# A message-passing layer on one core: layer 3 computed with edges on partitions, and 60 blocks selected by one-hots in place of 52

## What is computed

```python
x_j, x_i = x[src], x[dst]                       # (200000, 32) each
msg = concatenate([x_i, x_j - x_i], axis=-1)    # 64 columns
h = relu(msg @ W1 + b1)                         # W1 64x64
h = relu(h @ W2 + b2)                           # W2 64x128
h = relu(h @ W3 + b3)                           # W3 128x64
m = h @ W4 + b4                                 # W4 64x32
s = segment_sum(m, dst, 12500)
out = layernorm(x + s / maximum(cnt, 1)[:, None])
```

## Time and profile before

| | us |
|---|---|
| timed runs, median (lowest to highest) | 1571.46 (1568.09 to 1571.53) |
| the profiled execution: span from first to last instruction | 2441.1 |
| TensorE matmul busy in it | 1767.5 |
| VectorE busy | 947.9 |
| ScalarE busy | 602.6 |
| GpSimd busy | 1125.9 |
| mean granted clock of TensorE | 0.764 of full speed |

### The profile page before, as it was taken

How to read it: one execution, slowest core, us unless ns; L and a number is a source line. 1 busy time by engine, 2 the same in 40 slices (tenths; PEclk the granted TensorE clock), 3 DMA queues, 4 the chain that set the end, 5 groups by cost and what they waited for, 6 DMA issues and landing times.

```text
span 2441.1 us, 39243 instructions
## 1 busy us (share of the span) xinstructions
PE 1767.5 (72%) x13131; PEld 1040.0 (43%) x13131; DVE 947.9 (39%) x3086; ACT 602.6 (25%) x945; POOL 1125.9 (46%) x1165
## 2 busy tenths in 40 slices
PE   3133777777768777878787778786867778777797
PEld 2112444444444444444444444444444444444454
DVE  3663343333333343333333333443333333333356
ACT  2233122222212222212222222222221222122234
POOL 5275444453544454354545454544444454444411
PEclk7555787877878787777778877777877877787888
DMA  5334643343434443353434353544344344444332
GB/s 128 98 93 88 200 112 112 106 140 94 136 101 116 126 121 109 103 147 91 135 105 136 104 152 92 152 109 114 104 123 115 111 114 109 133 118 118 109 106 59
DMA packets 189929, 283.06 MB, mean 116 GB/s; under 512 B 84614, under 2 KB 90169, under 8 KB 189156
## 3 DMA queue, kind: packets, MB, share of 16 engines
q1 hardware_dynamic: 152341, 241.67, 33.7%
q0 software_dynamic: 36704, 37.00, 7.3%
q10 hardware_dynamic: 682, 1.85, 0.3%
HBM read 266.51 MB, written 13.73 MB: 115 GB/s over the span
## 4 chain that ended last, share of the span: by engine, by line
PE 63%; issue 23%; another core or an unknown queue 6%; DVE 3%; ACT 2%; DMA 1%; SPq 1%; DVEq 0%; POOL 0%; ACTq 0%; POOLq 0%
PE ps L964 22%; PE ps L996 12%; PE ps L988 10%; PE ps L1019 5%; PE ps L1004 4%; PE ps L919 3%; PE ps L901 3%; PE ps L1016 2%; PE ps L978 2%; ACT work L716 1%; ACT work L731 1%; DMA sums<-in_src 1%; DVE region L1410 0%; DVE region L1292 0%
## 5 line engine op out<-in xcount | busy, mean ns | idle before, releaser
L585 POOL DMA_INDIRECT xj<-z_rows,src_t x1107 | 1074.5, 971 | 1190.9 <-PE ps L919 787.7
L964 PE MATMUL ps<-region,x_p 128*96 128x150 bf16 (+53 forms) x5876 | 569.6, 243 | 416.6 <-issue 407.2
L964 PEld LDWEIGHTS ps<-region,x_p 128*96 128x96 bf16 x5876 | 440.6, 142 | 572.9 <-issue 566.7
L731 ACT ACTIVATE work<-ps,b3s 128x512 f32<-128x512 f32 x196 | 134.7, 687 | 1335.5 <-PE ps L996 1037.1
L996 PE MATMUL ps<-work,w3s 128*64 128x512 f32 x784 | 356.6, 840 | 21.2 <-issue 21.1
L1377 DVE TENSOR_SCALAR region<-region,cst 128x1565 bf16<-128x1565 int16 (+6 forms) x416 | 245.7, 634 | 268.0 <-remote 256.3
L988 PE MATMUL ps<-work,w2s 64*128 64x512 f32 x784 | 298.1, 827 | 6.8 <-ACT work L716 5.6
L724 ACT ACTIVATE work<-ps,b2s 128x512 f32<-128x512 f32 x392 | 250.7, 684 | 161.0 <-PE ps L988 82.7
L1392 DVE COPY work<-ps 128x512 f32<-128x512 f32 x194 | 133.4, 687 | 336.4 <-PE ps L1004 217.0
L1386 DVE CAST work<-ps 96x512 bf16<-96x512 f32 x52 | 35.7, 686 | 513.9 <-PE ps L964 506.8
L1410 DVE TENSOR_SCALAR region<-iota_g,dst_rel 128x42 f32<-128x42 f32 x1120 | 185.7, 250 | 0.0
(11 more groups left out here) (156 smaller groups left out, 826.3 us busy)
## 6 DMA issues: line engine op xcount, KB each, us to landing
dstb<-dst_rows SPq DMA_DIRECT2D x196, 252.0 KB
region<-src_rows SPq DMA_DIRECT2D x104, 391.2 KB
region<-src_rows SPq DMA_DIRECT2D x52, 407.2 KB
region<-src_rows SPq DMA_DIRECT2D x52, 403.2 KB
region<-src_rows SPq DMA_DIRECT2D x52, 376.2 KB
region<-src_rows SPq DMA_DIRECT2D x52, 375.8 KB
region<-src_rows SPq DMA_DIRECT2D x52, 374.0 KB
region<-src_rows SPq DMA_DIRECT2D x52, 366.2 KB
```

The lines of the kernel that those rows point to most:

```text
L585: pool.indirect_dma_start(out=xj[:, u, j % UT, j // UT, 0:w], out_offset=None, in_=rows, in_offset=bass.IndirectOffsetOnAxis(ap=cols[:, j: ...
L964: chosen = nc.tensor.matmul(ps[0:XP, XBANK[h], lo - h * UE:hi - h * UE], xb[:, a, :], hot[:, q % QN, at + lo:at + hi], start=not begun[h], ...
```

## The change

Layer 3's matmuls have their operands exchanged: the block's h2 tile (128 features x 128 edges) is loaded and the 64 columns of W3 are moved, so the result has edges on partitions at once. Eight such matmuls stand in place of two with 512 moved columns and of the four turning matmuls. They write one of two banks, by the block's parity. The bias b3 is now along the free axis, where ScalarE cannot add it, so relu(a + b3) is written as max(a, -b3) + b3: VectorE's copy becomes a maximum with a row that holds -b3 on every partition, and b3 through W4 is added once to the last layer's bias row, which the counts multiply. ScalarE's relu 3 and its first copies go. One step of distance goes too: the sum is now of block s-2 in step s, the one-hots are built for block s-1, and the addition stands directly behind the maximum on VectorE. SB grows from 52 to 60.

```diff
-SB = 52
+SB = 60
...
-        p_x, p_h1, p_h3 = ps[:, 0, :], ps[:, 1, :], ps[:, 4, :]
+        p_x, p_h1 = ps[:, 0, :], ps[:, 1, :]
         p_h2 = ps[:, 2:4, :]
-        p_ht = ps[:, 5, :]
+        p_h3 = ps[:, 4:6, :].rearrange("p v (t h f) -> p v t h f", t=UT, h=2)
+        p_b4 = ps[H3:H3 + 1, 7, 256:256 + O]
...
# sync: -b3 comes to all partitions
+            sp.dma_start(floor3[:, :], b3.unsqueeze(0).to_broadcast([P, H3])).then_inc(s_w, 16)
...
# scalar
-            def relu3(s):
-                v = s % 2
-                act.wait_ge(s_l3, 2 * (s + 1))
-                if s >= 2:
-                    act.wait_ge(s_ht, s - 1)
-                nc.scalar.activation(h3[:, v, :], p_h3, ACT.Relu, bias=b3s[:, 0:1]).then_inc(s_r3, 1)
...
# tensor
             def layer3(s):
-                if s >= 1:
-                    pe.wait_ge(s_r3, s)
+                if s >= 2:
+                    layer3_copied(pe, s - 2)
                 for h in range(2):
                     pe.wait_ge(s_r2[h], s + 1)
-                    nc.tensor.matmul(p_h3[h * H3:(h + 1) * H3, :], w3s[:, :], h2[:, s % 2, h, :],
-                                     start=True, stop=True).then_inc(s_l3, 1)
+                    for t in range(UT):
+                        made = nc.tensor.matmul(p_h3[:, s % 2, t, h, :], h2[:, s % 2, h, t * T:(t + 1) * T], w3s[:, :],
+                                                start=True, stop=True)
+                made.then_inc(s_l3, 1)
-
-            def turn_layer3(s):
...
-                stay_busy({S_N + 1: 3}.get(s, 0))
-                if 2 <= s <= S_N + 1:
-                    turn_layer3(s - 2)
-                stay_busy({S_N: 4, S_N + 1: 2, S_N + 2: 8}.get(s, 0))
-                if s >= 3:
-                    sum_window(s - 3)
+                stay_busy({S_N: 4, S_N + 1: 6}.get(s, 0))
+                if s >= 2:
+                    sum_window(s - 2)
...
+            nc.tensor.matmul(p_b4, b3s[0:H3, :], w4s[0:H3, :], start=True, stop=True).then_inc(s_b4, 1)
...
# vector
+                nc.vector.tensor_scalar(floor3[:, :], floor3[:, :], -1.0, None, ALU.mult).then_inc(s_ready, 1)
+
+            def last_weights():
+                dve.wait_ge(s_b4, 1)
+                link(nc.vector.tensor_tensor(w4s[H3:H3 + 1, :], w4s[H3:H3 + 1, :], p_b4, ALU.add))
...
             def copy_layer3(s):
-                dve.wait_ge(s_ht, s + 1)
+                dve.wait_ge(s_l3, s + 1)
                 if s >= 2:
                     dve.wait_ge(s_agg, s - 1)
...
-                nc.vector.tensor_copy(h3t[:, s % 2, :, :, 0:H3], p_ht.rearrange("p (t h f) -> p t h f", t=UT, h=2))\
+                nc.vector.tensor_tensor(h3t[:, s % 2, :, :, 0:H3], p_h3[:, s % 2, :, :, :],
+                                        floor3[:, :].unsqueeze(1).unsqueeze(1).to_broadcast([P, UT, 2, H3]), ALU.max)\
                     .then_inc(s_h3c, 1)
...
             def step(s):
+                if 2 <= s <= S_N + 1:
+                    copy_layer3(s - 2)
+                if s >= 3:
+                    add_sums(s - 3)
                 if s < S_N and is_sorted(s):
                     copy_x(s)
-                if AHEAD <= s <= S_N + 1:
-                    copy_layer3(s - 2)
                 if s + 1 < S_N:
                     build_pick(s + 1)
-                if 2 <= s <= S_N + 1:
-                    build_onehot(s - 2)
-                if s >= 3:
-                    add_sums(s - 3)
+                if 1 <= s <= S_N:
+                    build_onehot(s - 1)
```

More of the change, by code:

```diff
@@ L163, in build @@
         b3s = sb("b3s", [P, 1], F32)
+        floor3 = sb("floor3", [P, H3], F32)
         ring_at = 4 * PT * WIN + 4 * PE2
@@ L220, in build @@
         x16 = part(work[:, :].bitcast(BF16), 12 * UE, (2, UE))
-        h3 = part(work, 8 * UE, (2, UE))
         h3t = part(work, 10 * UE, (2, PT * (H3 + 1))).rearrange("p v (t h f) -> p v t h f", t=UT, h=2)
@@ L296, in build @@
         s_l2 = [sem(f"layer2_unit{n}") for n in range(2)]
-        s_l3, s_ht, s_agg = sem("layer3"), sem("layer3_turned"), sem("window_summed")
-        s_h3a = sem("layer3_copied_by_scalar")
+        s_l3, s_agg = sem("layer3"), sem("window_summed")
         s_pick, s_oh, s_h3c, s_acc = sem("pick_built"), sem("onehot_built"), sem("layer3_copied"), sem("sums_added")
@@ L301, in build @@
         s_moved, s_centre = sem("windows_moved"), sem("centring_chain")
-        s_r1, s_r3 = sem("relu1"), sem("relu3")
+        s_r1 = sem("relu1")
         s_r2 = [sem(f"relu2_unit{n}") for n in range(2)]
@@ L307, in build @@
         s_open = sem("pass_open")
+        s_b4 = sem("bias_through_w4")
         s_begun = sem("gathers_begun")
@@ L364, in layer3_copied @@
         def layer3_copied(eng, s):
-            if s < AHEAD - 2:
-                eng.wait_ge(s_h3a, s + 1)
-            else:
-                eng.wait_ge(s_h3c, s + 3 - AHEAD)
+            eng.wait_ge(s_h3c, s + 1)
         def even_rows(n):
@@ L683, in _ @@
                 split_more(g)
-            act.wait_ge(s_w, 15 * 16)
+            act.wait_ge(s_w, 16 * 16)
             act.wait_ge(s_set, 2)
@@ L722, in relu2 @@
                     if s >= 2:
[L723 removed]
+                        act.wait_ge(s_l3, s - 1)
                     nc.scalar.activation(h2[:, v, h, :], p_h2[:, h, :], ACT.Relu, bias=b2s[:, 0:1]).then_inc(s_r2[h], 1)
[L726 to L738 removed]
             def step(s):
@@ L991, in layer3 @@
             def layer3(s):
-                if s >= 1:
-                    pe.wait_ge(s_r3, s)
+                if s >= 2:
+                    layer3_copied(pe, s - 2)
                 for h in range(2):
                     pe.wait_ge(s_r2[h], s + 1)
-                    nc.tensor.matmul(p_h3[h * H3:(h + 1) * H3, :], w3s[:, :], h2[:, s % 2, h, :],
-                                     start=True, stop=True).then_inc(s_l3, 1)
-            def turn_layer3(s):
-                pe.wait_ge(s_r3, s + 1)
-                if s >= 1:
-                    layer3_copied(pe, s - 1)
-                for t in range(UT):
-                    turned = nc.tensor.transpose(p_ht[:, t * T:(t + 1) * T], h3[:, s % 2, t * T:(t + 1) * T], ident)
-                turned.then_inc(s_ht, 1)
+                    for t in range(UT):
+                        made = nc.tensor.matmul(p_h3[:, s % 2, t, h, :], h2[:, s % 2, h, t * T:(t + 1) * T], w3s[:, :],
+                                                start=True, stop=True)
+                made.then_inc(s_l3, 1)
             def sum_window(s):
@@ L1053, in _ @@
                 step(s)
+            pe.wait_ge(s_w, 16 * 16)
+            nc.tensor.matmul(p_b4, b3s[0:H3, :], w4s[0:H3, :], start=True, stop=True).then_inc(s_b4, 1)
             pe.wait_ge(s_widep, 2)
@@ L1064, in _ @@
                 turn_masked()
-                for s in range(AHEAD, S_N + 3):
+                for s in range(AHEAD, S_N + 2):
                     step(s)
@@ L1179, in weights @@
             def weights():
-                dve.wait_ge(s_w, 15 * 16)
+                dve.wait_ge(s_w, 16 * 16)
                 w = w1par[0:XP, :]
@@ L1185, in weights @@
                 nc.vector.tensor_tensor(w1p[0:XP, 2, :], w, w1p[0:XP, 1, :], ALU.subtract)
+                nc.vector.tensor_scalar(floor3[:, :], floor3[:, :], -1.0, None, ALU.mult).then_inc(s_ready, 1)
+            def last_weights():
+                dve.wait_ge(s_b4, 1)
+                link(nc.vector.tensor_tensor(w4s[H3:H3 + 1, :], w4s[H3:H3 + 1, :], p_b4, ALU.add))
                 link(nc.vector.tensor_reduce(w4mean[:, :], w4s[:, 0:O], AX.X, ALU.add))
                 link(nc.vector.tensor_scalar(w4mean[:, :], w4mean[:, :], -1.0 / O, None, ALU.mult))
-                nc.vector.tensor_scalar(w4s[:, 0:O], w4s[:, 0:O], w4mean[:, 0:1], None, ALU.add).then_inc(s_ready, 1)
+                link(nc.vector.tensor_scalar(w4s[:, 0:O], w4s[:, 0:O], w4mean[:, 0:1], None, ALU.add))
             def subtract_part0(h):
@@ L1388, in copy_layer3 @@
             def copy_layer3(s):
-                dve.wait_ge(s_ht, s + 1)
+                dve.wait_ge(s_l3, s + 1)
                 if s >= 2:
                     dve.wait_ge(s_agg, s - 1)
-                nc.vector.tensor_copy(h3t[:, s % 2, :, :, 0:H3], p_ht.rearrange("p (t h f) -> p t h f", t=UT, h=2))\
+                if s == 0:
+                    dve.wait_ge(s_ready, 1)
+                nc.vector.tensor_tensor(h3t[:, s % 2, :, :, 0:H3], p_h3[:, s % 2, :, :, :],
+                                        floor3[:, :].unsqueeze(1).unsqueeze(1).to_broadcast([P, UT, 2, H3]), ALU.max)\
                     .then_inc(s_h3c, 1)
@@ L1464, in _ @@
             count_passes()
+            last_weights()
             dve.wait_ge(s_end, 1)
```

10 lines of the change are left out of this document (removed).

## The result

The changed kernel takes 1610.99 us (median of 4 runs, 1601.77 to 1614.33), the kernel before in the same comparison 1569.83 us; the ratio is 1.026 [1.022, 1.030]. Forecast were 1552 us and a gain: the sign was wrong.

What follows compares the result with a forecast made beforehand. GpSimd's gathers were taken to bound the kernel before; after the change TensorE would, at 180 + 189 x 4.89 + 60 x 6.68 + 41 - 2 = 1544 us, plus 8 for a general shortfall: 1552 us, range 1500 to 1622.

Steps and rivals of the forecast that it cites:

- The recording was stretched: Profile of the kernel before: span 2441.1 us against 1571.46 timed, so durations can be taken from it, not the total.
- The 65 us of holding: GpSimd before the change: about half of 416 builds lengthen a gather by 0.31 us, 65 us on top of 1507.
- Layer 3's matmuls: TensorE, each step: the new group takes 1.89 us and replaces 1.52, so the step becomes 4.89 us, 0.37 slower.
- GpSimd's end: GpSimd after the change: 64 gathers fewer save 80 to 84 us, so it ends at 1487, or 1497 with holding.
- The one row of a long gather, 1.25 us: Trace of the kernel before: a gather beside a selection one-hot took 1.25 us in place of 0.94.
- TensorE's end, 1544 us: TensorE after the change: 180 + 189 x 4.89 + 60 x 6.68 + 41 - 2 = 1544 us, the new bound.
- the sum chain: TensorE's sum waits for VectorE's maximum, then additions: 1.83 us against 1.98 available, 0.15 us to spare.
- the first rival: VectorE late for the maximum so TensorE waits at the sum, or a general shortfall: 1577 to 1620 us, chance 0.29.
- the way to step 6: Time ahead of step 6 on TensorE: 255 us in the trace, less 36, 25 and 14 us of stretching, 180 us.
- Cheaper loads: Rival: layer 3's TensorE loads cost under 0.092 us, GpSimd stays the bound, 1485 to 1525 us, chance 0.16.
- Slow supply of instructions: Rival: TensorE's instructions arrive slowly in timed runs too, some 2500 more records, 1620 us and up, chance 0.08.
- one above 1580 that TensorE is held or that the shortfall is general: Sign: a time above 1580 us shows TensorE waiting, or the model's missing 42 us lying in all engines.

Runs made afterwards that it cites:

- the undisturbed recording: The kernel before, unchanged, profiled anew: 1567.04 us in one run, recorded span 1565.2 us.
- the additions first: Changed kernel with VectorE's additions ahead of the maximum: 1618.04 us with nothing else changed, 1562.71 us with the builds also set apart.
- two reorderings: Changed kernel with selection builds set apart on VectorE, 1585.26 us; with additions ahead of the maximum, 1618.04 us; with both, 1562.71 us.

## Why the prediction was wrong, point by point

*The recording was stretched, and GpSimd's gathers set the end before.* Right. The inferred 1.31 us for one gather is 1.30 in the undisturbed recording. The 65 us of holding are 60, but partly by luck: they were worked out as half of the builds holding 0.31 us each, and only 36 of the 60 fall on gathers that meet a build.

*Layer 3's matmuls.* Right in mechanism and size: 1.93 us for 1.89, and the step is longer without transposes (4.52 us, 4.86 where nothing waits, with the additions first).

*The step that failed: "GpSimd's end: 1571 - 84 = 1487, or 1497 with the holding", and with it "the bound passes from GpSimd to TensorE".* The saving was sized well, the holding not: 10 us more were forecast, 125 came (60 to 185). The one row of a long gather, 1.25 us, was taken as the price of meeting a build, and holding was scaled with the number of builds. The runs showed in its place that two or three builds in a row can hold a gather until the row ends (1.96 and 2.83 us), and that the total depends on where in a gather a row begins, which every change of order or pace moves: 60 us before, 118 with the layer 3 part alone, 145 with 60 blocks alone, 143 with the whole change and half of layer 3's matmuls left out, 185 with the whole change. GpSimd's end, forecast at 1497, was the 1611 measured. The order had already shown the additions moving away from between the one-hots and the builds; a row that begins between two gathers costs 0.3 us behind an addition and 1.4 behind the one-hots, but what this order costs alone was not separated from the longer step. The Trainium skill, "SBUF — State Buffer", section "Who interferes with whom", was cited for this lock in the prediction: an engine that is shut out waits for the whole instruction of the other. The traces agree as far as they can: gathers beside builds are longer, and a build that meets a gather takes 0.74 to 0.79 us in place of 0.60. That a whole row of builds can shut GpSimd out is this case's finding. The forecast had the direction and not the size.

*TensorE's end, 1544 us.* Too low by 41: with the gathers cut by an eighth the kernel takes 1585. Of this 23 us are the sum chain. The forecast gave it 0.15 us to spare; in the trace TensorE comes to the sum 0.2 us too soon, since 0.80 us (1017.06 to 1017.86) and not 0.61 lie between the maximum's start and the addition, and the maximum starts 0.11 us behind layer 2, not 0.08. That was the first rival. Its range of 1577 to 1620 holds the 1611 measured by luck, since GpSimd put the end there; TensorE's own end, 1585, lies in it by the rival's reason and would have turned the sign without GpSimd (1585 against 1565). The sum chain is what turns it: without it TensorE ends at 1563. Some 10 us are the selected blocks (0.17 us in three steps, 60 times), 2 the way to step 6, and some 6 are not accounted for. Two errors nearly cancelled in the way to step 6: the forecast read 180 us off the stretched recording where the kernel before has 168, and it put the going of ScalarE's first copies at nothing, where the layer 3 part of the change made the way 14 us longer, to 182. What was to hide it was ScalarE's idle time; but the work went to VectorE, which was merging keys.

*The other rivals.* Cheaper loads, excluded by the 1.93 us. Slow supply of instructions, excluded: with the additions first TensorE ran 13449 records in 1200 us without a gap.

*The range* of 1500 to 1622 holds 1611, by luck too: no part of the forecast had GpSimd as the bound above 1525 us, and the sign "one above 1580 that TensorE is held or that the shortfall is general" left this case out. The sign that the recorded span would grow to 2700 us failed too: this recording was paced like the timed runs.

## What to carry to other kernels

When a change takes work off the engine that sets the end, price what the other engines' new instructions do to the duration of the ones that stay. For instructions that lock each other out take a range, from nothing to the longest row that can form, not the single case that the trace happens to show: here the same kind of row cost 0 or 1.88 us, by 0.12 us in its start, and only a run gives the total. Setting the builds apart helped in one kernel (185 to 95 us of holding) and hurt in the other (60 to 90). Where two engines end within some per cent of each other, an edit to one alone may show nothing or a loss: here two reorderings were worth nothing and 26 us apart and 48 together. When an operation is handed to another engine, look at that engine's queue in the first steps, not only in the steady ones.

## What the runs showed of the hardware beyond that

The same kernel recorded twice had spans of 2441.1 and 1565.2 us, with TensorE's instructions arriving 0.7 us apart in the first while 39 of the same kind, behind 999.60 us, took 2.42 us together in the second. Durations of single instructions agree between them (0.94 us for a gather, 0.69 for a 512-column copy on VectorE); waits and totals do not.

The exclusion goes both ways. In the kernel before the builds are longer in the mean (660 ns, against 617 in the changed kernel), and there they hold the gathers less:

```profile
L1377 DVE TENSOR_SCALAR region<-region,cst 128x1565 bf16<-128x1565 int16 (+6 forms) x416 | 252.9, 660 | 12.0 <-DMA region<-src_rows 11.0
```

What stands directly ahead of a row on VectorE goes with what it costs. Of the rows of three that begin in the 0.30 us between two gathers, those behind an addition cost 0.34 us at most in the kernel before (58 rows), and 0.35 at most for 48 of 50 with 60 blocks; those behind the one-hots cost 1.36 to 1.56 us, each of 88 rows in four runs (the changed kernel, its run with 52 blocks, the one with half of layer 3's matmuls, the one with the additions first). Why this is so was not settled, nor why so many rows of the changed kernel begin 0.32 to 0.34 us into a gather.
